# Causal attention scores in two fp32r parts on the two halves of TensorE's rows, with every row tile masked in the maximum

## What is computed

```python
q = (x @ Wqa @ Wqb).reshape(b, s, 16, 16)          # 16 heads of 16
kv = (x @ Wkva @ Wkvb).reshape(b, s, 4, 16, 2)     # 4 key heads, each shared by 4 query heads
k, v = (kv[..., 0], kv[..., 1])
q, k = _rope(q), _rope(k)
scores = jnp.einsum('bqhd,bkhd->bhqk', q, k) * 16 ** -0.5
scores = jnp.where(causal, -jnp.inf, scores)
w = jax.nn.softmax(scores, axis=-1)
out = jnp.einsum('bhqk,bkhd->bqhd', w, v).reshape(b, s, E)
return out @ Wout + bout
```

## Time and profile before

| | |
|---|---|
| median of 3 runs | 1352.33 us (1351.51, 1352.33; the third 3423.91) |
| the profiled execution | 1347.93 us, its span 1346.2 us |
| busy over the span | PE 1057.0 us (79%), DVE 783.6, ACT 661.9, POOL 342.8 |
| mean granted TensorE clock | 0.905 |
| attention, from its block to the last values | about 151 to 506 us |

### The profile page before, as it was taken

How to read it: one execution, slowest core, us unless ns; L and a number is a source line. 1 busy time by engine, 2 the same in 40 slices (tenths; PEclk the granted TensorE clock), 3 DMA queues, 4 the chain that set the end, 5 groups by cost and what they waited for, 6 DMA issues and landing times. The chain is left out here.

```text
span 1346.2 us, 22491 instructions
## 1 busy us (share of the span) xinstructions
PE 1057.0 (79%) x6813; PEld 764.0 (57%) x6813; DVE 783.6 (58%) x1685; ACT 661.9 (49%) x1166; POOL 342.8 (25%) x524
## 2 busy tenths in 40 slices
PE   3766068788999984892566999999998999998875
PEld 2444023343444433772454877878787787877764
DVE  4888356576777743864344664746556474655523
ACT  1334115466666673461224456473755747364433
POOL 0443136566333331010111120403012040301200
PEclk9777558899999996896677999999999999999987
DMA  2332423333222103357102030301203030020000
GB/s 85 106 113 78 133 87 119 105 117 113 91 88 96 58 33 128 133 224 265 47 12 98 1 125 0 109 16 40 84 0 115 10 109 16 0 78 1 15 1 16
DMA packets 52156, 103.20 MB, mean 77 GB/s; under 512 B 6584, under 2 KB 31936, under 8 KB 48000
## 3 DMA queue, kind: packets, MB, share of 16 engines
q1 hardware_dynamic: 48924, 95.02, 20.6%
q0 software_dynamic: 1920, 6.03, 1.4%
q10 hardware_dynamic: 1252, 1.39, 0.3%
HBM read 62.45 MB, written 39.58 MB: 76 GB/s over the span
## 5 line engine op out<-in xcount | busy, mean ns | idle before, releaser
L804 ACT ACTIVATE p_probs<-p_psS 128x512 f32<-128x512 f32 (+1 forms) x352 | 180.7, 564 | 121.5 <-ACTq L803 119.1
L706 DVE CUSTOM_DVE_ANT_0 p_psA<-p_psA,p_mask 128x512 f32<-128x512 f32 (+1 forms) x256 | 155.6, 647 | 103.5 <-DVEq L704 103.1
L1744 DVE TENSOR_TENSOR p_hl<-p_h,p_hh 128x512 fp32r<-128x512 f32 x128 | 86.9, 688 | 156.2 <-DVEq L1743 154.2
L838 PE MATMUL p_psA<-p_ks,p_qs 96*128 96x512 bf16 (+3 forms) x512 | 144.1, 317 | 36.7 <-PEq L836 36.4
L857 PE MATMUL p_psS<-p_qs,p_ks 99*128 99x256 bf16 (+3 forms) x512 | 130.6, 308 | 19.6 <-PEq L882 11.3
L1629 ACT ACTIVATE p_h<-p_psG,w_columns 128x512 f32<-128x512 f32 x128 | 88.2, 689 | 100.3 <-ACTq L1628 99.9
L868 PE MATMUL p_psO<-p_probs,p_v 128*32 128x512 f32 (+3 forms) x1024 | 92.2, 454 | 27.5 <-PEq L864 26.8
L725 POOL TENSOR_SCALAR_AFFINE_SELECT p_probs<-p_probs 128x512 f32<-128x512 f32 x128 | 80.6, 634 | 129.6 <-POOLq L724 112.4
L1597 POOL TENSOR_TENSOR p_base<-p_x,p_q 128x1024 f32<-128x1024 f32 x8 | 20.0, 2502 | 363.1 <-POOLq L1596 352.9
L1955 PE MATMUL p_psY<-p_n,p_hh 128*128 128x256 f32 x512 | 105.8, 290 | 2.7 <-PEq L2015 2.3
L857 PEld LDWEIGHTS p_psS<-p_qs,p_ks 99*128 99x128 bf16 x512 | 43.6, 98 | 105.7 <-issue 90.7
(11 more groups left out here) (247 smaller groups left out, 2750.7 us busy)
## 6 DMA issues: line engine op xcount, KB each, us to landing
p_n<-n_parts SPq DMA_DIRECT2D x16, 1024.0 KB, 6.7
o_sums<-p_o SPq DMA_DIRECT2D x32, 256.0 KB, 2.9
n_parts<-p_nh SPq DMA_DIRECT2D x8, 1024.0 KB, 3.9
n_parts<-p_nl SPq DMA_DIRECT2D x8, 1024.0 KB, 6.0
q_parts<-p_part SPq DMA_DIRECT2D x48, 128.0 KB
p_qs<-q_parts SPq DMA_DIRECT2D x32, 192.0 KB
p_x<-in_x_dram SPq DMA_DIRECT2D x8, 512.0 KB, 3.9
p_qs<-q_parts SPq DMA_DIRECT2D x32, 128.0 KB
```

What stands on the lines that cost most here:

```text
L706: nc.vector.tensor_tensor_reduce(out=bank[:, 0:w], in0=bank[:, 0:w], in1=mask[:, S - w:S], scale=1.0, scalar=MASKED, op0=ALU.add, op1=ALU.max,
L804: nc.scalar.activation(probs[:, g % 2, at:at + n * w], psS[place(s, turn) % SB][:, 0:n * w], ACT.Exp, scale=SCALE).then_inc(exp_done, 1)
L838: last = nc.tensor.matmul(bank[:, z * w:(z + 1) * w], qs[0:SROWS, k, g * G + r0 + z, i * P:(i + 1) * P], ks[0:SROWS, k, g, 0:w], start=Tru ...
L1744: nc.vector.tensor_tensor(hl[:, s, :], h[:, s, :], hh[:, s, :].bitcast(F32), ALU.subtract).then_inc(h_parts, 1)
```

## The change

`project_phase` keeps two fp32r parts of `rot` instead of three bf16 ones: ACT rounds the first, DVE subtracts for the second. Three of the four products remain (hi hi, hi lo, lo hi): 48 rows instead of 96. The parts are stored in fp32 words, the doubled one twice. Even heads lie in partitions 0 to 49, odd heads in 64 to 113 of `qs` (48 rows and 2 for the maxima); `ks` is held twice. A matmul then uses rows 0-63 or 64-127 of the array. All 16 row tiles of a group are units of their own, masked in DVE's maximum; no mask matmuls are left. Two heads of the same parity share one matmul where they fit in 512 columns. The units are ordered so that a column unit and the row units beside it lie on opposite halves. The values of tile 0 stand one step later, and the maxima use the free end of a column unit's bank.

```diff
-PAIRS = [(0, 0), (0, 1), (0, 2), (1, 0), (1, 1), (2, 0)]
-PARTS = 3
-SROWS = len(PAIRS) * D
-MROWS = 3
+Q_PARTS = (0, 0, 1)
+K_PARTS = (0, 1, 0)
+SROWS = len(Q_PARTS) * D
+MROWS = 2
+HALF = P // 2
...
-        rem = sb("rem", [P, RING, S], F32)
-        part = [sb(f"part{i}", [P, RING, S], BF16) for i in range(3)]
+        part = [sb(f"part{i}", [P, RING, S], F32R) for i in range(2)]
...
-                        nc.vector.tensor_tensor(rem[0:rows, n], rot[0:rows, n], part[0][0:rows, n],
-                                                ALU.subtract).then_inc(rem_ready, 1)
-                    if step >= 3:
...
-                        nc.vector.tensor_tensor(part[2][0:rows, n], rem[0:rows, n], part[1][0:rows, n],
+                        nc.vector.tensor_tensor(part[1][0:rows, n], rot[0:rows, n], part[0][0:rows, n].bitcast(F32),
                                                 ALU.subtract).then_inc(parts_ready, 1)
...
-                        nc.scalar.activation(part[1][0:rows, n], rem[0:rows, n], ACT.Copy).then_inc(mid_ready, 1)
...
-        qs = sb("qs", [P, 2, H, S], BF16)
-        ks = sb("ks", [P, 2, KVH, S], BF16)
+        qs = sb("qs", [P, 2, H // 2, S], F32R)
+        ks = sb("ks", [P, 2, KVH, S], F32R)
...
-        PV0_AT, PV1_AT = 7, 10
-        SUNITS = [(0, r, 1) for r in range(G)] + [(1, r, 1) for r in range(G)] + [(2, 0, 2), (2, 2, 2), (3, 0, 4)]
+        PV0_AT, PV1_AT = 8, 11
+        SUNITS = [(0, (0,)), (0, (2,)), (0, (1,)), (0, (3,)), (1, (1,)), (1, (3,)), (1, (0,)), (1, (2,)),
+                  (2, (0, 2)), (2, (1, 3)), (3, (1, 3)), (3, (0, 2))]
-        AUNITS = [(3, 0, 1), (2, 0, 1), (3, 1, 1), (2, 1, 1), (1, 0, 2), (3, 2, 1), (2, 2, 1), (3, 3, 1), (2, 3, 1),
-                  (1, 2, 2), (0, 0, 4)]
+        AUNITS = [(3, (1,)), (2, (1,)), (3, (0,)), (2, (0,)), (3, (2,)), (2, (2,)), (3, (3,)), (2, (3,)),
+                  (1, (1,)), (0, (3,)), (1, (0,)), (0, (2,)), (1, (2,)), (0, (0,)), (1, (3,)), (0, (1,))]
-        ROWS_AT = list(range(11))
+        ROWS_AT = [0, 1, 2, 3, 4, 5, 6, 7, 8, 8, 9, 9, 10, 10, 11, 11]
...
+            for e in range(2):
+                queue.dma_start(ks[e * HALF:e * HALF + SROWS, k, two].rearrange("p g t -> p (g t)").bitcast(F32),
+                                scr["k"][:, :, b, two].rearrange("i d g t -> (i d) (g t)")).then_inc(kv_in[k][z], 16)
...
+                for e in range(2):
+                    sp.dma_start(qs[e * HALF:e * HALF + SROWS, k, g * G // 2:(g + 1) * G // 2, :].bitcast(F32),
+                                 scr["q"][:, :, b, :, :].rearrange("i d (h e) t -> (i d) e h t", e=2)[:, e, g * G // 2:(g + 1) * G // 2]
                                  ).then_inc(q_in[k][g], 16)
...
         def _(dve):
+            for e in range(2):
+                nc.vector.memset(ks[e * HALF + 32:(e + 1) * HALF].bitcast(F32), -1.0).then_inc(minus_set, 1)
...
-            nc.vector.memset(ks[SROWS:P, :, :, :], -1.0).then_inc(minus_set, 1)
...
-                    if n == 1:
-                        nc.vector.tensor_tensor_reduce(out=bank[:, 0:w], in0=bank[:, 0:w], in1=mask[:, S - w:S], scale=1.0,
-                                                       scalar=MASKED, op0=ALU.add, op1=ALU.max,
-                                                       accum_out=mx[:, h, i:i + 1]).then_inc(A_free, 1)
-                    else:
-                        nc.vector.tensor_reduce(mx[:, h:h + n, i], bank[:, 0:n * w].rearrange("p (r k) -> p r k", r=n), AX_X,
-                                                ALU.max).then_inc(A_free, 1)
+                    nc.vector.tensor_tensor_reduce(out=bank[:, 0:w], in0=bank[:, 0:w], in1=mask[:, S - w:S], scale=1.0,
+                                                   scalar=MASKED, op0=ALU.add, op1=ALU.max,
+                                                   accum_out=mx[:, h, i:i + 1]).then_inc(A_free, 1)
...
         def _(act):
+            act.wait_ge(minus_set, 2)
+            act.sem_inc(minus_set, -2)
             for k in range(2):
                 for z in range(2):
                     load_keys(act, k, k, z)
...
-                for z in range(n):
-                    last = nc.tensor.matmul(bank[:, z * w:(z + 1) * w], qs[0:SROWS, k, g * G + r0 + z, i * P:(i + 1) * P],
-                                            ks[0:SROWS, k, g, 0:w], start=True, stop=(n == 1))
-                    if n > 1:
-                        last = nc.tensor.matmul(bank[:, z * w + i * P:(z + 1) * w], ident_b[:, :], mask_b[:, :], start=False, stop=True)
+                for z, r in enumerate(heads):
+                    rows = slice(r % 2 * HALF, r % 2 * HALF + SROWS)
+                    last = nc.tensor.matmul(bank[:, z * w:(z + 1) * w], qs[rows, k, (g * G + r) // 2, i * P:(i + 1) * P],
+                                            ks[rows, k, g, 0:w], start=True, stop=True)
```

More of the change, by code:

```diff
@@ L310, in pair @@
             def pair(ahead):
-                for step in range(RING + 3):
+                for step in range(RING + 2):
                     if step < RING:
@@ L319, in pair @@
                         nc.vector.engine_nop().then_inc(XR_free, 1)
-                    if 2 <= step < RING + 2:
+                    if step >= 2:
                         n = step - 2
@@ L396, in pair @@
             def pair(ahead):
-                for step in range(RING + 2):
+                for step in range(RING + 1):
                     if step < RING:
@@ L728, in split @@
             def split(g):
-                rows = mx[:, g * G:(g + 1) * G, :].rearrange("p h t -> p (h t)")
-                hi, mid, low = (msplit[:, g, i, :] for i in range(MROWS))
+                rows = mx[:, g * G:(g + 1) * G, :].rearrange("p (r e) t -> p e r t", e=2)
+                hi, low = (msplit[:, g, :, i] for i in range(MROWS))
                 pool.wait_ge(maxima_done, 1)
@@ L788, in maxima @@
             def maxima(bank, g):
-                act.wait_ge(S_ready, 1)
-                act.sem_inc(S_ready, -1)
-                nc.scalar.activation(mrows[:, g, :], bank[0:MROWS * NG, 0:P], ACT.Copy).then_inc(exp_done, 1)
+                nc.scalar.activation(mrows[:, g, :], bank[0:MROWS * NG, S - P:S], ACT.Copy)
                 act.drain().then_inc(m_ready, 1)
@@ L846, in maxima @@
                 pe.sem_inc(split_ready, -1)
-                nc.tensor.matmul(bank[0:MROWS * NG, 0:P], msplit[:, g].rearrange("p i x -> p (i x)"), ident_b[:, :],
-                                 start=True, stop=True).then_inc(S_ready, 1)
+                return nc.tensor.transpose(bank[0:MROWS * NG, S - P:S], msplit[:, g].rearrange("p e i r t -> p (e i r t)").bitcast(F32),
+                                           ident[:, :])
             def score_cols(bank, k, g, s):
-                j, r0, n = SUNITS[s]
-                w = widths[j]
-                key = ks[0:SROWS + MROWS, k, g, j * P:(j + 1) * P]
-                for z in range(n):
-                    h = g * G + r0 + z
-                    last = nc.tensor.matmul(bank[:, z * w:(z + 1) * w], key, qs[0:SROWS + MROWS, k, h, j * P:S],
-                                            start=True, stop=True)
-                last.then_inc(S_ready, 1)
+                j, heads = SUNITS[s]
+                w, n, e = widths[j], len(heads), heads[0] % 2
+                rows = slice(e * HALF, e * HALF + SROWS + MROWS)
+                first = (g * G + heads[0]) // 2
+                nc.tensor.matmul(bank[:, 0:n * w].rearrange("p (r q) -> p r q", r=n), ks[rows, k, g, j * P:(j + 1) * P],
+                                 qs[rows, k, first:first + n, j * P:S], start=True, stop=True).then_inc(S_ready, 1)
             def values(k, g, j):
```

132 lines of the change are left out of this document (50 added, 82 removed).

## The result

The changed kernel takes **1443.51 us** (median of 4 runs, 1437.46 to 1447.04) against 1352.68 for the kernel before (median of 4 runs, three at 1351.51 to 1353.03): a ratio of 1.0664, with a 95% interval of 1.0631 to 1.0696. The fourth run of the kernel before took 3423.91 us, and the ratio is formed without it. The change makes the kernel slower by 91 us where 53 us of gain were forecast, and the time lies outside the range. The profiled execution took 1447.04 us; its span is 1445.2 us against 1346.2 before.

A forecast was written before the change was run, and what follows sets the result against it. PE was taken to bound the attention, 8.41 of 9.10 us a group. Gains of 27 (steady groups), 5 (early groups), 12 (projection) and 9 (start), 53 us, gave 1294.9, plus 4.4: 1299 us, range 1275 to 1322.

The forecast's parts named there:

- the sum's silent term: Attention: PE durations at 2.4 GHz kept for the new matmuls; a fall to 1.2 GHz was named only as a risk.
- Two halves at once: Attention scores on PE: matmuls on rows 0-63 and 64-127 overlap fully, cutting PE's demand some 1.9 us to 6.5 a group.
- What is late next: Attention behind PE: DVE at 7.3 and ACT at 7.4 us make a group 7.8 us, bounds 7.2 and 8.4.
- Masks, -0.48 us a group: Attention on PE: eight mask matmuls leave each group, taking 0.48 us off PE.
- fp32r, +0.66 us a group: Attention on PE: 28 fp32r matmuls cost slightly more, +0.42 us, and four of 128 columns +0.24 us a group.
- Projection, -12 us: Projection: fewer DVE subtractions and one ACT rounding less save 3 us a pair, 12 us (5 to 18); larger stores uncharged.
- rival B: Projection and attention start: halves overlap, but larger stores bound a pair and keys come late; 1320 us, chance 0.11.
- Start of the attention, -9 us: Wait ahead of the first maxima: evenly spread loads shorten it by 9 us, bounds +5 and -12.
- the settings of -1: Attention start: done twice, 7 to 8.5 us, with ACT's key loads waiting for both; most of it taken as hidden.
- The tail: Attention start: a few DMA engines' late query loads; without it 14 us shrink to about 3, -11 us.
- Rival C: Attention on PE: each change of halves exposes some 0.10 us, 84 us on top of no overlap; 1413 us, chance 0.09.

The follow-up runs named there:

- e1_rows112: Changed kernel with every score matmul on 112 or 116 rows, both halves in each, leaving out the separation of heads: 1372.12 us.
- e2_one_half: Changed kernel with all heads' score matmuls on rows 0 to 49, one half alone, leaving out the odd heads' scores: 1516.30 us.
- e3_bf16_48: Kernel before with three bf16 products instead of six, so scores use 48 and 51 rows: 1548.46 us.
- e5_fill12: Changed kernel with one idle 512-column bf16 matmul on all 128 rows ahead of each of a group's 12 column units: 1411.77 us.
- e10_blocks3: Changed kernel with one idle full-row matmul ahead of column units 0, 3 and 9, three a group: 1422.50 us.
- e4_no_masks: Kernel before, bf16 scores kept, with 16 row units masked in the maximum, no mask matmuls, in an order of its own: 1367.83 us, ratio 1.0104.
- e11_pad16_two: e7_pad_two with the change's 16 row units, masked inside the maximum, instead of 11 with mask matmuls: 1332.31 us, ratio 0.9857 to the kernel before.
- e7_pad_two: Changed kernel with scores on 96 to 100 rows, zeros in the keys, old masked row units, two parts stored: 1332.94 us, ratio 0.9871 to the kernel before.
- e8_after_two: Changed kernel with two projection parts stored instead of three, the copy made by twice as many loads: 1422.39 us.
- e9_blocks12: Changed kernel with 12 idle full-row matmuls a group in blocks of four ahead of column units 0, 3 and 9: 1477.81 us.

## Why the prediction was wrong, by its own steps

- **The step that failed** is the sum's silent term: durations at 2.4 GHz were carried over to matmuls that use half of the array. I had the risk in the last sentence, but as "PE, with more idle time, falls to 1.2 GHz", and gave it no price and no chance. PE did not idle; it had the lower clock while busy for 104 of 110 us. What the runs show in its place is the rows: score matmuls on 48 to 51 rows, in one half, come with half the clock, those on 96 and more with the full one. This is shown by e1_rows112, e2_one_half and e3_bf16_48, and by e5_fill12 from the other side. It costs more than 32 us: e5_fill12 is that much faster although it spends 12 x 0.32 = 3.8 us a group on idle matmuls. From the 13.06 us of a group of the change to the 10.07 of e10_blocks3 at the full clock it is 3.0 us a group, some 90 us in all (an estimate), about the whole loss.
- **Two halves at once**: right, as a mechanism, at both clocks. The size was too high: I took 1.9 us of PE's time at the full clock; at half the clock, where that would be 3.8, it saved 2.1 us a group. At the full clock the group of e10_blocks3 has 8.76 us of PE with 0.96 of filler, 7.8 instead of the 6.5 of the forecast.
- **What is late next**: the forecast of 7.8 us a group would have failed at the full clock as well. DVE's units have the price that the slope gave (7.7 us busy against 7.3). But the two chains meeting in PE's order cost more than the 0.4 us allowed: a group takes 10.07 us with fillers, 9.1 without them (an estimate from e10_blocks3), and 9.73 in bf16 with nothing overlapped, where the old order had 9.11.
- **Masks, -0.48 us a group**: PE's work fell and the group did not (e4_no_masks +0.6 us, e11_pad16_two +0.02 to e7_pad_two). The step took PE's work for the group's time; on all rows it turned into waits. The 0.6 us of e4_no_masks belong to an order of units that the change does not have.
- **fp32r, +0.66 us a group**: too low with masks, where PE is busy for 9.5 us of a group of e7_pad_two against 8.4 in bf16; not too low without them, as in the change: 9.0 us (e11_pad16_two, 419.00 to 428.92) against 8.6 (e4_no_masks). The sum left out what an fp32r score costs behind another kind of matmul. Behind the values, four times a group, it is 0.33 to 0.34 us to the next one in e7_pad_two (as 420.95 to 421.28) against 0.22 to 0.23 (as 425.19 to 425.41). Behind a bf16 mask a score of 256 columns takes 0.20 us instead of 0.12 (e7_pad_two, 418.76 to 418.96 and 418.60 to 418.72).
- **Projection, -12 us**: the working on DVE was right (the last part was ready 11 us earlier), but the stores end the stage, as rival B had it: the stores end 6.5 us later than before. I had the amount right and said that the queues "could carry about 320" GB/s; from 135 to 150 us, when nothing but the stores runs, they carry 159 at a share of 0.47. e8_after_two shows the price: 17 us.
- **Start of the attention, -9 us**: from SP's first load to the first column unit 34.5 us now (157.68 to 192.16) against 40.4 before (151.15 to 191.51), 5.9 gained. From the load to the first row unit it takes 16.6 us against 15.8, so the settings of -1 were mostly hidden, as forecast. The tail shrank less than the 11 us taken: from the first copy of maxima to the first column unit 8.1 us against 14.8. That loads of 48 rows spread more evenly was not tested. With the late stores nothing of the gain is left.
- **Rival C** was the nearest in its number (1413) and wrong in its mechanism, so the nearness is luck: pairs on changing halves follow each other every 0.19 us in e10_blocks3. What costs is going between the fillers on the whole array and the pairs on halves, about 0.1 and 0.2 us in e5_fill12. The Trainium skill ("TensorEngine Tiling (Array Packing)", Overview, Key Properties) says that a change of tiling mode drains the engine; the runs agree in that going over costs these 0.1 and 0.2 us, and cannot tell whether by a drain.
- Had the clock held, the attention at 9.1 to 10.07 us a group would have taken 282 to 312 us instead of 315.4, and the whole, with the 7.4 us of the start, 1327 to 1357 us (an estimate from e10_blocks3): even then not the 1299 of the forecast.

## What to carry to other kernels

Read the granted clock before any duration, and ask of each edit what it does to the rows that TensorE's matmuls use. Here packing two heads into halves of the array saved PE some time and came with half its clock, and laying two heads on 96 rows, with zeros in the keys at the other head's rows, brought it back. Price an edit at each engine's order as well as at its work: in e4_no_masks PE was 88% and DVE 78% busy, and the group still got longer. When a projection's compute shrinks and its stores grow, take the end of the stores as the end of the stage.

## What the runs showed of the hardware that was not expected

- The granted clock was 0.50 with PE busy for 110.00 of 110 us, in bf16 and in fp32r, when the score matmuls used 48 to 51 rows, and 1.00 with PE busy for 99.58 when they used 112 and 116. The Trainium skill ("TensorE: Matmul & The Clock Gate", Part 1) makes the clock depend on how busy PE has been; the measurement decides here, and in it the busy share alone does not settle the clock.
- The same 12 idle matmuls a group gave a clock of 1.00 when spread over the steps and 0.88 in three blocks of four (e9_blocks12, 290 to 502.5 us), and 3 of them 0.84 and 0.67 (e10_blocks3, 290 to 400 and 400 to 502.5 us), with groups of 10.07 and of 14.68 us in one run.
- At the full clock two fp32r matmuls on different halves follow each other in pairs every 0.19 to 0.33 us; going from the whole array to halves exposes about 0.1 us and more. The same 0.11 us shows in fp32r on 96 to 100 rows behind the values (e7_pad_two) and not in bf16 (before), and 0.08 us behind a bf16 mask on the whole array. So the change of tile may not be all of it; what makes it up is open.
